# The last attention of four: PV with the probabilities as the stationary operand, and the division behind it

## The chip, the core and the metric

The kernel runs on one core of one Trainium2 chip. The metric is the device time of one launch in microseconds. Five engines work side by side: PE (TensorE), DVE (VectorE), ACT (ScalarE), POOL (GpSimd) and SP (SyncE, which issues the DMAs).

## The reference, cut to what matters

Four cross-attention layers run one after the other on `x` (8, 128, 256) and a context of the same shape. The change touches only the fourth, which has 16 heads of width 16, 128 queries and 128 keys for each of 8 sequences:

```python
x = layer_norm(hidden_states, ln1_w, ln1_b)
q = (x @ q_w + q_b).reshape(B, LQ, H, HD).transpose(0, 2, 1, 3)
k = (encoder_hidden_states @ k_w + k_b)...
v = (encoder_hidden_states @ v_w + v_b)...
scores = jnp.einsum('bhqd,bhkd->bhqk', q, k) * scale
scores = jnp.where(mask, scores, mask_value)
attn = jax.nn.softmax(scores, axis=-1)
out = jnp.einsum('bhqk,bhkd->bhqd', attn, v)
out = out.transpose(0, 2, 1, 3).reshape(B, LQ, D)
out = out @ cproj_w + cproj_b
hidden = out + residual
y = layer_norm(hidden, ln2_w, ln2_b)
y = jax.nn.gelu(y @ fc_w + fc_b, approximate=True)
return hidden + (y @ proj_w + proj_b)
```

Everything is in float32. Dense products are made from a rounded high part and a low part of each operand, three matmuls per product (`three`, L762 to L766).

## The kernel before, in words

Every engine has a program of its own and walks the same list of events; semaphores tie the engines together. The list of the fourth layer ("L3") is written by `att_order("L3")` (L171 to L248). Its unit u is one S event: four heads of one sequence. There are 32 units: 4 iterations (two sequences each) of 4 steps (four heads) of 2 units (the sequence). In the order of a unit u, for w = u - 5:

- S(u): PE makes the scores of four heads in one of two PSUM banks (L895 to L901), DVE takes the negated row maximum (L1609), ACT takes exp per head, with the row sum in its accumulator (L1270), DVE takes the reciprocal of the sums (L1560, for the unit before), and POOL multiplies the 128x512 probabilities by it (L1857).
- T(u - 3): PE transposes the four heads (L909), ACT (even) or DVE (odd) copies them to `probT` (L1281, L1622).
- PV(w): PE multiplies, four products of a stationary 128x32 slice of the values (`vt`, 16 columns of it filled) and 128 moving columns of `probT`, into the 32-row strips of an output bank (L932). The result is transposed already, channels in rows.
- OUT(it), right behind the last PV of an iteration: ACT copies the bank to the high part `uu[0]` (L1287), DVE writes the low part (L1625).
- WO(it), two units later (`WO_LATE`; directly in the next unit after the last iteration): PE makes the output projection in a general bank, DVE adds it to the residual `X` and takes the statistics of the next norm (L1631, L1481).
- For the next steps: "pq" and "pk" (stacked queries and keys, L851 to L861, copied by ACT L1252 and L1262 and DVE L1606, the other key rows by DMA L679), and for the next iteration "dk", "dq", "dv" in units 3, 5 and 9 of an iteration (dense projections; ACT L1246, DVE L1578, values DVE L1592).
- Then further events, written with `put` (L191 to L207): parts of the MLP weights ("w", ACT L1201, DVE L1471), the norm in front of the MLP ("nS", "nX", "nT"), and the first MLP groups: ("up", 0, 0) in unit 32, ("up", 0, 1) in unit 33, ("up", 0, 2) in unit 36. An "up" is 12 matmuls on PE, a gelu on ACT (L1365), and the high and low parts on DVE (L1713, L1714).

Dense products, stackings, projections and norm transposes ("general" users) share two PSUM banks in turn (`j_bank`, `j_take`). The waits for a bank to be freed sit in PE's program ahead of the user's first matmul. DVE walks the list through `late` (L260 to L275): up to the last S, the kinds named in `LATE["L3"]` are done behind the next S event; after the last S the list holds as written. `SEAM_COVER` fills PE with matmuls on the identity ahead of a norm's transposes; only `norm_step` calls `cover` (L786).

The MLP of the layer follows ("L3" of `mlp_order`, L366 to L375): ("up", 0, 3), ("up", 1, 0), the first "down" and the second half of the norm, which needs the WO of all iterations.

## Time and profile before

| | us |
|---|---|
| median of 3 runs | 1174.37 (1172.15 to 1174.82) |
| the profiled execution's own time | 1175.04 |
| its span in the trace | 1173.2 |
| PE busy | 1062.5 (91%) |
| DVE busy | 727.7 (62%) |
| ACT busy | 715.2 (61%) |
| POOL busy | 317.5 (27%) |

The span is what the trace covers; the execution's own time has 1.8 us around it. The shares are means over four layers with different limits, so a change in one layer is read from that layer's stretch. The fourth layer's first S runs near 1016 us, its last PV at 1119.5 us, and its MLP ends the program. In the views, a busy PE counts a matmul up to its modelled end, so matmuls that follow each other overlap in the records. In a timeline the columns are start, duration, engine, line, operation, output and input names, shape and count; a bracket gives the idle time before and what ended it.

### The profile page before, as it was taken

The page shows a single profiled execution, that of the slowest core. Times are in us where ns is not written, and L with a number is a line of the kernel's source. Part 1 is how long each engine was busy: PE and PEld are TensorE (multiplying, and loading weights), DVE is VectorE, ACT ScalarE, POOL GpSimd, SP SyncE. Part 2 cuts the span into 40 slices and gives each one's busy share as a digit, 9 for nine tenths or more (in the row PEclk, how much of TensorE's full clock was granted, in tenths as well). Part 3 has the DMA queues.
Part 4 walks back from the last instruction along what each step waited for, and adds up shares of the span by engine and source line. Part 5 has one row for each costly group of instructions (what it writes and reads, how often), then busy time and mean ns, then how long its engine had stood idle before and what let it go on. Part 6 is the DMA issues. An engine that isn't in the chain of part 4 may idle for free.

```text
span 1173.2 us, 24063 instructions
## 1 busy us (share of the span) xinstructions
PE 1062.5 (91%) x8248; PEld 936.7 (80%) x8248; DVE 727.7 (62%) x1747; ACT 715.2 (61%) x2080; POOL 317.5 (27%) x440
## 2 busy tenths in 40 slices
PE   7998897789978999999998989999999989778788
PEld 5776675677758979999998868999998979667588
DVE  7777574667886645555555645555555585667773
ACT  2776765677884456666655546666665452689852
POOL 5232543756540012211111103111112112143311
PEclk9999899899999999999999999999999999899899
DMA  5211011011101021111001101011111110100100
GB/s 171 66 46 41 22 43 33 15 23 27 45 20 53 19 90 46 46 46 46 19 29 68 46 1 57 35 46 46 46 46 37 37 54 1 48 18 19 48 10 28
DMA packets 29853, 48.09 MB, mean 41 GB/s; under 512 B 6627, under 2 KB 20389, under 8 KB 29734
## 3 DMA queue, kind: packets, MB, share of 16 engines
q1 hardware_dynamic: 29638, 46.49, 12.7%
q8 instruction: 68, 1.11, 0.4%
q14 instruction: 51, 0.42, 0.1%
q10 hardware_dynamic: 96, 0.07, 0.0%
HBM read 36.54 MB, written 1.05 MB: 32 GB/s over the span
## 4 chain that ended last, share of the span: by engine, by line
PE 66%; DVE 12%; ACT 10%; issue 7%; POOL 2%; SPq 1%; DMA 1%; ACTq 0%; DVEq 0%; POOLq 0%
PE ps L764 14%; PE ps L765 14%; PE ps L766 14%; PE ps L1008 4%; PE ps L984 4%; PE ps L1146 3%; ACT pt L1270 2%; PE ps L993 2%; PE ps L909 2%; DVE nm L1806 2%; PE ps L1133 1%; PE ps L1124 1%; PE ps L932 1%; DVE nmax L1609 1%; POOL pt L1857 1%
## 5 line engine op out<-in xcount | busy, mean ns | idle before, releaser
L1857 POOL TENSOR_TENSOR pt<-pt,prec 128x256 f32<-128x256 f32 (+1 forms) x224 | 180.8, 808 | 628.2 <-DVE prec L1678 500.4
L1325 ACT ACTIVATE pt<-ps,nmax 128x129 f32<-128x129 f32 x256 | 92.1, 366 | 101.0 <-DVE nmax L1670 100.2
L764 PE MATMUL ps<-rs 128*128 128x256 f32 x480 | 142.8, 298 | 4.1 <-DVE rs L1692 2.8
L1471 DVE TENSOR_TENSOR rs<-wraw,rs 128x256 fp32r<-128x256 f32 (+2 forms) x116 | 68.8, 595 | 124.5 <-ACT rs L1201 124.1
L765 PE MATMUL ps<-rs 128*128 128x256 f32 x480 | 135.9, 283 | 0.0
L766 PE MATMUL ps<-rs 128*128 128x256 f32 x480 | 135.8, 283 | 0.0
L1270 ACT ACTIVATE pt<-ps,nmax 128x256 f32<-128x256 f32 (+1 forms) x256 | 105.1, 423 | 42.6 <-DVE nmax L1609 42.3
L764 PE MATMUL ps<-ht,rs 128*128 128x256 f32 (+1 forms) x304 | 107.6, 354 | 9.0 <-DVE ht L1521 3.0
L766 PE MATMUL ps<-ht,rs 128*128 128x256 f32 (+1 forms) x304 | 101.4, 333 | 0.0
L765 PE MATMUL ps<-ht,rs 128*128 128x256 f32 (+1 forms) x304 | 101.3, 333 | 0.0
L764 PEld LDWEIGHTS ps<-rs 128*128 128x128 f32 x480 | 91.8, 191 | 7.9 <-DVE rs L1692 4.8
L1692 DVE SCALAR_TENSOR_TENSOR rs<-ps,col,rs 128x256 fp32r<-128x256 f32 x128 | 61.9, 484 | 53.1 <-ACT rs L1342 53.1
L765 PEld LDWEIGHTS ps<-rs 128*128 128x128 f32 x480 | 92.0, 192 | 0.0
L766 PEld LDWEIGHTS ps<-rs 128*128 128x128 f32 x480 | 91.9, 191 | 0.0
L764 PE MATMUL ps<-rs,ct 128*128 128x256 f32 x288 | 86.4, 300 | 3.4 <-ACT rs L1252 1.5
L1806 DVE TENSOR_REDUCE nm<-ps 128x2 f32<-128x512 f32 x128 | 82.1, 679 | 7.0 <-PE ps L1124 7.0
L1609 DVE TENSOR_REDUCE nmax<-ps 128x2 f32<-128x512 f32 (+1 forms) x96 | 65.6, 684 | 29.3 <-PE ps L899 21.9
L984 PEld LDWEIGHTS ps<-fs 128*128 128x128 f32 x512 | 75.7, 190 | 10.1
L1365 ACT ACTIVATE fs<-ps,col 128x256 f32<-128x256 f32 x96 | 40.2, 471 | 68.4 <-PE ps L766 67.3
L1413 ACT ACTIVATE pt<-ps 128x512 f32<-128x512 f32 x128 | 73.1, 599 | 14.2 <-PE ps L1133 12.2
L765 PE MATMUL ps<-rs,ct 128*128 128x256 f32 x288 | 80.9, 281 | 0.0
L766 PE MATMUL ps<-rs,ct 128*128 128x256 f32 x288 | 80.9, 281 | 0.0
(206 smaller groups left out, 2998.8 us busy)
## 6 DMA issues: line engine op xcount, KB each, us to landing
wraw<-in_packs SPq DMA_DIRECT2D x52, 512.0 KB, 3.8
rs<-rs SPq DMA_DIRECT2D x222, 32.0 KB, 1.9
bvr<-in_l2rows SPq DMA_DIRECT2D x16, 256.0 KB, 4.6
rs<-rs SPq DMA_DIRECT2D x96, 16.0 KB
row<-in_rows SPq DMA_DIRECT2D x2, 640.0 KB, 4.9
XH<-in_packs SPq DMA_DIRECT2D x2, 512.0 KB, 4.0
out<-X SPq DMA_DIRECT2D x4, 256.0 KB, 2.1
X<-in_x SPq DMA_DIRECT2D x3, 256.0 KB, 3.3
```

The source lines that it names most:

```text
L764: nc.tensor.matmul(dst, w[0], m[1], start=start, stop=False)
L765: nc.tensor.matmul(dst, w[1], m[0], start=False, stop=False)
L766: return nc.tensor.matmul(dst, w[0], m[0], start=False, stop=stop)
L984: last = nc.tensor.matmul(ps[:, S_BANK + g % 2, b * D:b * D + P + 1], qT[:, hh % 3, 2 * b2 + b, :], kT[:, hh % 3, 2 * b2 + b, :], start=Tr ...
L1270: last = nc.scalar.activation(prob[:, i % PROBS, h * keys:(h + 1) * keys], ps[:, SCORE_BANKS[ph][i % len(SCORE_BANKS[ph])], h * keys:(h + ...
L1325: last = nc.scalar.activation(prob[:, g % PROBS, k * D:k * D + P + 1], ps[:, S_BANK + g % 2, k * D:k * D + P + 1], ACT.Exp, bias=nmax[:, g ...
L1413: nc.scalar.activation(pt[:, i % L0_PTS, :], ps[:, L0_X[i % len(L0_X)], :], ACT.Exp, scale=Q0_SCALE).then_inc(Z["ex"], 1)
L1471: last = nc.vector.tensor_tensor(dst[1], src, f32(dst[0]), ALU.subtract)
L1609: nc.vector.tensor_reduce(nmax[:, i % 4, 0:nh], ps[:, SCORE_BANKS[ph][i % len(SCORE_BANKS[ph])], :].rearrange("p (h n) -> p h n", h=nh), A ...
L1692: nc.vector.scalar_tensor_tensor(cc[1][:, hd, two, :], ps[:, O_BANK + g % 2, 0:D].rearrange("p (b n) -> p b n", b=2), C(f"L2bv{p // PAIRS ...
L1806: nc.vector.tensor_reduce(nm[:, s % 3, im, 2 * p:2 * p + 2], ps[:, L0_S[i % len(L0_S)], :].rearrange("p (h n) -> p h n", h=2), AX.X, ALU.m ...
L1857: nc.gpsimd.tensor_tensor(pr, pr, prec[:, u % 4, 0:nh].unsqueeze(2).broadcast_to([P, nh, keys]), ALU.mult)\
```

## The change

The row sum is no longer taken by ACT and no longer divided out before the transposes. T waits for exp. The values get a column of ones behind their 16 columns. In PV `probT` of a head (128 keys x 128 queries) is the stationary operand and 17 columns of `vt` move; the result has queries in rows and holds the row sum as its 17th column. A new event NO, one unit behind every second PV, is done by DVE: a reciprocal of 8 sums per row and one multiplication of two sequences' four heads into `attn`. OUT becomes four transposes of `attn` on PE into a general bank, in front of ACT's copy and DVE's subtraction; it is two units later than before for the first three iterations and one unit later, behind the last NO, for the last. WO is two units later for the first three iterations, one unit for the last. POOL waits for exp ahead of its row additions. Two entries of `SEAM_COVER` go.

```diff
-SEAM_COVER = {("nT", "L2nm", 0): 5, ("nT", "L2nm", 2): 6, ("pq", "L3", 0): 6, ("S", "L3", 2): 9}
+SEAM_COVER = {("nT", "L2nm", 0): 5, ("nT", "L2nm", 2): 6}
...
             yield ("PV", w // U)
-            if w % per_it == per_it - 1:
+            if ph == "L1" and w % per_it == per_it - 1:
                 yield ("OUT", w // per_it)
+        if ph == "L3" and 2 <= w <= total and w % 2 == 0:
+            yield ("NO", w // 2 - 1)
+        for it in range(c["iters"] if ph == "L3" else 0):
+            if w == (it + 1) * per_it + (2 if it + 1 < c["iters"] else 0):
+                yield ("OUT", it)
...
-            if w == (it + 1) * per_it + ((WO_LATE if ph == "L3" else 1) if it + 1 < c["iters"] else 0):
+            if w == (it + 1) * per_it + (4 if ph == "L3" and it + 1 < c["iters"] else 1 if ph == "L3" or it + 1 < c["iters"] else 0):
                 yield ("WO", it)
...
+        def sums(s):
+            return ps[:, O_BANK + s % 2, 0:2 * P].rearrange("p (m q c) -> p m q c", m=2, q=4)
...
-                    pe.wait_ge(a["nm"], i + 1)
+                    pe.wait_ge(a["nm" if ph == "L1" else "ex"], i + 1)
...
+                elif e == "PV" and ph == "L3":
+                    it, r = divmod(i, 2 * STEPS)
+                    m, im = divmod(r, 2)
+                    copied(pe, ph, i)
+                    if r == 0:
+                        pe.wait_ge(a["vals"], it + 1)
+                    if i >= 4 and im == 0:
+                        pe.wait_ge(a["nm"], i // 2 - 1)
+                    for q in range(4):
+                        last = nc.tensor.matmul(sums(i // 2)[:, im, q, 0:HD + 1], probT[:, i % 3, q * P:(q + 1) * P],
+                                                vt[:, it % 2, im, 0, 4 * m + q, 0:HD + 1], start=True, stop=True)
+                    last.then_inc(a["pm"], 1)
+                elif e == "OUT" and ph == "L3":
+                    pe.wait_ge(a["nm"], STEPS * (i + 1))
+                    bank = j_bank()
+                    for im in range(2):
+                        for t in range(2):
+                            last = nc.tensor.transpose(bank[:, (2 * im + t) * P:(2 * im + t + 1) * P], attn[:, i % 2, im, t * P:(t + 1) * P],
+                                                       ident[:, :])
+                    j_full(last, (a["oeA"], i + 1), (a["oeD"], i + 1))
...
+                            last = nc.scalar.activation(p_h, s_h, ACT.Exp, bias=nmax[:, i % 4, h:h + 1])
...
+                        if ph == "L3":
+                            last = nc.vector.tensor_tensor(vt[:, i % 2, s, 0, :, 0:HD],
+                                                           bank[:, s * D:(s + 1) * D].rearrange("p (h d) -> p h d", d=HD),
+                                                           R("L3v").rearrange("p (h d) -> p h d", d=HD), ALU.add)
+                            continue
...
-                    if i >= 1:
+                    if ph == "L1" and i >= 1:
                         reciprocal(i - 1)
...
+                elif e == "NO":
+                    it, m = divmod(i, STEPS)
+                    dve.wait_ge(a["pm"], 2 * i + 2)
+                    if m == 0 and it >= 2:
+                        dve.wait_ge(a["oeA"], it - 1)
+                    rc = prec[:, 2 * (i % 2):2 * (i % 2) + 2, 0:4]
+                    link(nc.vector.reciprocal(rc, sums(i)[:, :, :, HD]))
+                    dst = attn[:, it % 2, :, m // 2 * P:(m // 2 + 1) * P].rearrange("p m (q e d) -> p e m q d", q=4, e=2)[:, m % 2, :, :, :]
+                    nc.vector.tensor_tensor(dst, sums(i)[:, :, :, 0:HD], rc.unsqueeze(3).broadcast_to([P, 2, 4, HD]),
+                                            ALU.mult).then_inc(a["nm"], 1)
...
                 if e == "S":
-                    normalise(a, i, 4 // U, keys, keys)
+                    if ph == "L1":
+                        normalise(a, i, 4 // U, keys, keys)
...
                     if ph == "L3" and 1 <= i <= B:
+                        pool.wait_ge(a["ex"], i)
                         add_row(X, "L3o", i - 1)
...
-                part = nc.gpsimd.memset(fs[:, 512 * b:512 * (b + 1)], 0.0)
-            part.then_inc(vzero, 1)
+                if b < 2:
+                    ones = nc.gpsimd.memset(vt[:, b, :, 0, :, HD], 1.0)
+                if b == 1:
+                    ones.then_inc(vzero, 1)
```

## Rows read from the trace of the kernel before

**Rows 1.** Busy time by window over the last attention and the start of its MLP.
```profile
core 0: us, PE busy (x) PEld busy (x) DVE busy (x) ACT busy (x) POOL busy (x), PEclk, DMA share, GB/s
1027.00:1098.30 71.30, 60.28 (x577) 48.58 (x575) 50.49 (x122) 62.31 (x255) 30.41 (x32) 1.00 0.12 27
1098.30:1102.60 4.30, 0.07 (x5) 0.07 (x1) 3.21 (x8) 4.29 (x16) 1.04 (x1) 0.74 0.02 5
1102.60:1119.50 16.90, 12.85 (x116) 10.38 (x116) 12.94 (x23) 12.02 (x38) 3.49 (x3) 0.86 0.09 32
```

**Rows 2.** Timeline of PE: a stall, and one unit without.
```profile
1059.97 0.74 PE L851 MATMUL ps<-rs,sel 128*128 128x256 f32 x4 [1.32 <-DVE rs L1578]
...
1061.15 0.60 PE L909 MATMUL ps<-ident,pt 128*128 128x128 f32 x4
1061.68 0.42 PE L932 MATMUL ps<-pt,fs 128*32 128x128 f32 x8
1062.04 0.38 PE L764 MATMUL ps<-rs 128*128 128x256 f32 x1
```

**Rows 3.** Groups by line and shape, 1027 to 1098.3: busy us, mean ns, idle before.
```profile
L1857 POOL TENSOR_TENSOR pt<-pt,prec 128x512 f32<-128x512 f32 x25 | 26.0, 1040 | 40.1 <-DVE prec L1560 40.1
L1270 ACT ACTIVATION_READ_ACCUMULATOR pt<-ps,nmax 128x1 f32 x97 | 20.0, 206 | 0.0
...
L932 PE MATMUL ps<-pt,fs 128*32 128x128 f32 x200 | 10.6, 285 | 0.0
...
L1560 DVE RECIPROCAL prec<-psums 128x4 f32<-128x4 f32 x25 | 4.2, 168 | 0.3 <-ACT pt L1270 0.3
...
L1592 DVE TENSOR_TENSOR fs<-ps,row 128x128 f32<-128x128 f32 x12 | 2.6, 275 | 0.0
```

**Rows 4.** Timeline of the weight loads, at 39.8 us and at 706.6 us.
```profile
39.81 0.30 PEld L1114 LDWEIGHTS ps<-rs 128*128 128x128 f32 x2 [0.66 <-issue]
...
706.59 0.53 PEld L1008 LDWEIGHTS ps<-pt,fs 128*128 128x128 f32 x4
```

**Rows 5.** Timeline of ACT: exp of two heads of one unit.
```profile
1062.07 0.37 ACT L1270 ACTIVATE pt<-ps,nmax 128x128 f32<-128x128 f32 x1
1062.34 0.19 ACT L1270 ACTIVATION_READ_ACCUMULATOR pt<-ps,nmax 128x1 f32 x1
1062.43 0.36 ACT L1270 ACTIVATE pt<-ps,nmax 128x128 f32<-128x128 f32 x1
```

**Rows 6.** Timeline of DVE and POOL: one form alone, and beside a division.
```profile
1051.29 0.41 DVE L1520 CAST ht<-XH 128x512 fp32r<-128x512 f32 x1
...
1108.96 1.41 POOL L1857 TENSOR_TENSOR pt<-pt,prec 128x512 f32<-128x512 f32 x1 [0.75 <-DVE prec L1560]
...
1109.39 1.26 DVE L1520 CAST ht<-XH 128x512 fp32r<-128x512 f32 x1
```

**Rows 7.** Timeline of ACT, DVE and PE around the stall at 1098.3.
```profile
1100.68 0.60 ACT L1287 CAST rs<-ps 128x512 fp32r<-128x512 f32 x1
...
1101.31 0.69 DVE L1625 TENSOR_TENSOR rs<-ps,rs 128x512 fp32r<-128x512 f32 x1 [0.30 <-ACT rs L1287]
...
1102.56 0.77 PE L899 MATMUL ps<-rs 128*128 128x256 f32 x2 [4.23 <-DVE rs L1606]
```

**Rows 8.** Timelines of PE, ACT and DVE from the last PV to the last WO.
```profile
1119.52 0.43 PE L932 MATMUL ps<-pt,fs 128*32 128x128 f32 x8 [2.31 <-DVE pt L1622]
1121.84 0.41 PE L764 MATMUL ps<-rs 128*128 128x256 f32 x1
...
1120.02 0.59 ACT L1287 CAST rs<-ps 128x512 fp32r<-128x512 f32 x1 [2.43 <-PE ps L932]
1122.08 0.84 ACT L1365 ACTIVATE fs<-ps,col 128x256 f32<-128x256 f32 x2 [1.48 <-PE ps L766]
...
1122.95 0.43 DVE L1713 CAST rs<-fs 128x512 fp32r<-128x512 f32 x1 [1.63 <-ACT fs L1365]
1123.41 1.11 DVE L1714 TENSOR_TENSOR rs<-fs,rs 128x512 fp32r<-128x512 f32 x1
```

More of the change, by code:

```diff
@@ L33 @@
 H = 16
+HD = D // H
 DK2 = 128
@@ L81 @@
 PROBS = 4
-WO_LATE = 5 - T_LAG
 TE_ACT = {"L1": 2, "L3": 2}
@@ L512, in build @@
         assert o2 <= o
+        attn, _ = carve(fs, o, [2, 2, D])
         ms, o = carve(fs, o, [2, B, D])
@@ L1269, in att @@
                     for h in range(nh):
-                        last = nc.scalar.activation(prob[:, i % PROBS, h * keys:(h + 1) * keys],
-                                                    ps[:, SCORE_BANKS[ph][i % len(SCORE_BANKS[ph])], h * keys:(h + 1) * keys], ACT.Exp,
-                                                    bias=nmax[:, i % 4, h:h + 1], accum_out=psums[:, i % 4, h:h + 1])
+                        p_h = prob[:, i % PROBS, h * keys:(h + 1) * keys]
+                        s_h = ps[:, SCORE_BANKS[ph][i % len(SCORE_BANKS[ph])], h * keys:(h + 1) * keys]
+                        if ph == "L1":
+                            last = nc.scalar.activation(p_h, s_h, ACT.Exp, bias=nmax[:, i % 4, h:h + 1], accum_out=psums[:, i % 4, h:h + 1])
+                        else:
+                            last = nc.scalar.activation(p_h, s_h, ACT.Exp, bias=nmax[:, i % 4, h:h + 1])
                     last.then_inc(a["ex"], 1)
@@ L1282, in att @@
                 elif e == "OUT":
-                    act.wait_ge(a["pm"], 2 * STEPS * (i + 1))
-                    bank = ps[:, OUT_BANKS[ph][i % len(OUT_BANKS[ph])], :]
+                    if ph == "L1":
+                        act.wait_ge(a["pm"], 2 * STEPS * (i + 1))
+                        bank = ps[:, OUT_BANKS[ph][i % len(OUT_BANKS[ph])], :]
+                    else:
+                        bank = j_take()
                     if i > 0:
@@ L1585, in att @@
                     for s in range(2):
-                        im, t = (k[0], s) if ph == "L1" else (s, 0)
+                        if ph == "L3":
[3 more added lines that the diff above has]
+                            continue
+                        im, t = k[0], s
                         src = bank[:, s * D:(s + 1) * D].rearrange("p (t e q d) -> p e t q d", t=2, e=2, q=4)
@@ L1610, in att @@
                                             AX.X, ALU.max, negate=True).then_inc(a["mx"], 1)
-                    if i >= 1:
+                    if ph == "L1" and i >= 1:
                         reciprocal(i - 1)
-                    if i == total - 1:
+                    if ph == "L1" and i == total - 1:
                         reciprocal(i)
+                elif e == "NO":
[8 more added lines that the diff above has]
+                                            ALU.mult).then_inc(a["nm"], 1)
                 elif e == "T":
@@ L1623, in att @@
                 elif e == "OUT":
+                    bank = ps[:, OUT_BANKS[ph][i % len(OUT_BANKS[ph])], :] if ph == "L1" else j_take()
                     dve.wait_ge(a["oeA"], i + 1)
-                    nc.vector.tensor_tensor(uu[1].rearrange("p m t n -> p (m t n)"), ps[:, OUT_BANKS[ph][i % len(OUT_BANKS[ph])], :],
+                    nc.vector.tensor_tensor(uu[1].rearrange("p m t n -> p (m t n)"), bank,
                                             f32(uu[0].rearrange("p m t n -> p (m t n)")), ALU.subtract).then_inc(a["oeD"], 1)
@@ L1871, in att @@
                 if e == "S":
-                    normalise(a, i, 4 // U, keys, keys)
+                    if ph == "L1":
+                        normalise(a, i, 4 // U, keys, keys)
                     if ph == "L1" and i in (4, 14):
```

## The prediction

> **What bounds the kernel now.** I looked first at the table of windows over the last attention [rows 1]. In its steady part (1027 to 1098.3 us) ACT is busy 62.3 of 71.3 us, PE 60.3, DVE 50.5, POOL 30.4, at the full TensorE clock (1.00): no engine is saturated, and ACT is nearest. PE has 71.3 - 60.3 = 11.0 us of idle there. The reader should see two near-bounds side by side: relief for ACT is worth something only as far as PE has room, and work added to PE is free only as far as it falls into those 11.0 us. The PE timeline shows how a unit runs: four transposes (L909), PV (L932), then dense or stacking matmuls, back to back until a bank is missing; the last row of the group is one such stall, 1.32 us for DVE's low part of the dense projection (L1578) [rows 2]. None of these stalls ends with POOL: POOL waits for the reciprocal, and T is issued three units behind S, so the division on POOL (1.04 us a unit [rows 3]) is hidden.
>
> **PE: PV with the probabilities stationary.** Both versions issue four products a unit, and the profile has two records for each (200 L932 records for 25 units [rows 3]). Before, eight records on 32-column tiles overlap: from the first transpose (1061.15) to the first matmul behind PV (1062.04) is 0.89 us, of which the four transposes, 0.60 us less one record of some 0.28 for three of them, are 0.43 to 0.44; so PV costs 0.45 [rows 2]. After, each record has a 128-column weight load and only 17 moving columns. No row has 17 columns. The nearest are 128 columns: a pair of weight loads of L1114 takes 0.30 us with 0.19 for one, so they follow each other at 0.11; four of L1008, the same operand type as here, follow at (0.53 - 0.19) / 3 = 0.113 [rows 4]. L1114 streams half the columns of its neighbours and gets no closer together, so I read this as the price of the load, not of the stream. I take 8 x 0.109 = 0.87 us, just under these: 0.42 more per unit. The bounds are 8 x 0.12 = 0.96 above, and the old 0.45 below (no dearer at all).
> The Trainium skill ("TensorE: Matmul & The Clock Gate", section Back-to-back issue gap) puts a matmul of 1 to 64 columns at some 25 ns; by that alone PV would take about 0.2 us and the change would relieve PE. The same page's section LDWEIGHTS prices a load by its columns, 128 / 1.2 = 107 ns, which is what the rows of weight loads show; these govern here.
> The new OUT step is four transposes, 0.44 us, in each of four iterations, and it takes a general bank.
>
> **ACT.** Exp of one head starts at 1062.07, its accumulator read at 1062.34, the next head's exp at 1062.43: the read takes a slot of 0.09 us [rows 5], which goes with it. Per unit that is 4 x 0.09 = 0.35 us less. Bounds: 0 and 0.8 (the whole 0.206 of the accumulator rows, four times [rows 3]).
>
> **DVE and POOL.** Removed: 32 reciprocals of 0.17 us, two per step. Added per step: a reciprocal (0.17), a linked wait (some 0.1), a 128x128 multiplication from PSUM (0.28, as L1592) [rows 3]. So DVE gains about 0.2 us a step of work and loses its waits for exp; the values' bias goes from four instructions to two. I cost all this at nothing in the steady part, covered by PE; if DVE were the bound it would be 16 x 0.2 = 3.2. The queue position is what matters at the end, below. POOL's 1.04 us divisions go: DVE's L1520 takes 0.41 us alone and 1.26 where a division lies beside it [rows 6], so each such meeting gives back up to 0.85.
> The Trainium skill ("SBUF — State Buffer", section SBUF: two separate sides) says that GpSimd and such VectorE instructions exclude each other on a shared pair of ports for a whole instruction; the trace agrees (1.26 against 0.41). It speaks for the change, and only where DVE holds the path.
> The later T wait (exp in place of the division), POOL's added wait for exp before its row additions (nothing urgent queues behind it), the two small memsets instead of eight (POOL was idle there), and the two deleted cover entries, whose events never call that function, cost 0.
>
> **The sum,** against the profiled execution of 1175.04 us:
> - Steady part: 25 PV x 0.42 + 2 OUT x 0.44 = +11.4 us of PE work. What falls into the 11.0 us of idle is free. Most stalls are a wait for ACT or DVE with a PV between cause and effect, so each absorbs 0.42, plus 0.35 where an exp stands ahead of the copy that frees the bank. I take 9.0 absorbed, net +2.4 (bounds: half absorbed, +5.9; all, +0.4).
> - WO of an iteration now falls in the same unit as the next dv, two dense groups on two banks: +0.3 (0 to 1.8, a stall of 0.9 twice).
> - The stall at 1098.3: its chain on ACT loses one exp saving (0.35) and the OUT copy (0.60), on DVE the OUT subtraction [rows 7]: -1.2 (0 to -2.2, if PE then keeps its clock, 0.74 in this stretch and 0.86 in the next [rows 1]).
> - 1102.6 to 1119.5: five or six dearer PVs and an OUT against its idle of 4 us (16.9 - 12.85 [rows 1]) and one meeting with POOL less (-0.85): +0.8 (-1.5 to +3).
> - The end. The last PV is issued in unit 36, followed by the third MLP group ("up", 0, 2), whose conversion on DVE waits for its gelu. Before, OUT of the last iteration stood ahead of that: ACT's copy (1120.02) and DVE's subtraction were done while PE ran the MLP group, and WO started at once (1121.84) [rows 8]. After, the division ("NO", 15) and OUT are listed in unit 37. DVE is in order, so the division waits behind L1713 and L1714, which wait for the gelu: from the end of the MLP group, gelu ready 1.1 us on, conversions to 1124.52, 2.7 us on [rows 8]; then division 0.6, PE transposes with their latency 0.7, ACT copy 0.6, subtraction 0.7. WO starts 5.3 us behind the group instead of 0. All of the later MLP stands behind WO on PE, so it all moves. Plus 0.4 for the PV, less 0.7 for a weight conversion that now fits into the wait: +5.0 (+3 to +7, as PE may restart at half clock).
> Total 2.4 + 0.3 - 1.2 + 0.8 + 5.0 = +7.3: 1182.3. The median before is 0.67 below the profiled execution, so I forecast **1181.7 us**.
>
> **Rivals.**
> (A) *ACT is the bound, and the end is covered.* For it: ACT has the highest share [rows 1]. Then PE's stalls shrink further. PE's own work limits it: the 60.3 us hold at each stall a matmul's tail of some 0.17 us (a record of 0.28 less a spacing of 0.11); with some 19 stalls that is 3.2, so 57.1 + 11.4 = 68.5 is the least for the steady part, -2.8. With -2.2 at the stall, -1.5 after it and only +3.0 at the end, -3.5: 1170.9. It decides if the stalls vanish altogether; against it stand the waits for DVE, which gets no relief. 0.10.
> (B) *The short matmuls are cheap* (the issue rule above): PV at about 8 x 0.06 = 0.48, PE gains nothing and loses nothing. Then the steady part gains about half of ACT's 25 x 0.35 = 8.8, -4.4; with -1.2, -0.8 and +4.6 the sum is -1.8: 1172.6. Against it: the weight loads [rows 4]. 0.08.
> (C) *The gain and the loss cancel,* end +3, the rest 0 to -3: 1174 to 1177. 0.09.
> (D) *The clock.* With PV's streaming shortened and a 4 us hole at the end, PE falls to 1.2 GHz in part of the attention; each 5 us of PE work at that level costs 5 more. The clock held 1.00 through the steady part with 11 us idle, and fell only around the 4.3 us hole [rows 1]. +15 or more: above 1189. 0.05.
> (E) The forecast, slower by work on PE and by the late division: 0.68.
>
> **Numbers.** About 0.2% (2.3 us) is what a measurement of this kernel can tell from no change. Faster takes most of (A) and (B) and some of (C): 0.15; same 0.10; slower 0.75. The range leaves out (D) and the far side of (A): 1172.5 to 1189.5. Its lower part is B's and C's, its upper part the bounds of the steady part and the end.
>
> **What would show it.** PE's PV group at 0.85 to 0.95 us a unit (right) or near 0.45 (B); no accumulator reads in the last attention, ACT's exp at 0.26 a head; the PE idle of the steady part down from 11 to 2 to 4 us and its length up by 2 to 3; the stall near 1098 a microsecond shorter; and, clearest, a hole on PE of four to five microseconds in front of the last WO, ended by the OUT copy and subtraction, with DVE's multiplication started only after the third gelu's conversion. If that hole is missing, or PV stays at 0.45, the prediction is wrong.

## The result, and the profile after

| | before | after |
|---|---|---|
| median, us | 1173.26 (4 runs) | 1190.16 (4 runs, 1188.77 to 1196.17) |
| ratio to before | | 1.0156 [1.0115, 1.0198] |
| the profiled execution's own time | 1175.04 | 1191.27 |
| its span | 1173.2 | 1189.5 |
| mean granted TensorE clock | 0.978 | 0.967 |

The changed kernel is 16.9 us slower; 8.4 were forecast against this median, and the upper end of the range (1189.5) is missed by 0.7. The work around the change is the same, but some line numbers move: L764 to L766 of before are L773 to L775, L851 is L860, L858 is L867, L899 (S) is L908, L909 (T) is L918, L1287 is L1322, L1365 (gelu) is L1400, L1578 is L1613, L1592 is L1622, L1625 is L1675, L1713 and L1714 are L1763 and L1764. PV is L930, NO's reciprocal and multiplication L1660 and L1662, OUT's transposes L938.

The first view to read is the table of windows of the changed kernel, cut where the clock changes. Its columns are those of [rows 1].

```profile
core 0: us, PE busy (x) PEld busy (x) DVE busy (x) ACT busy (x) POOL busy (x), PEclk, DMA share, GB/s
1023.50:1033.00 9.50, 7.73 (x63) 7.25 (x63) 5.44 (x10) 7.42 (x21) 2.21 (x3) 0.99 0.07 14
1033.00:1046.30 13.30, 13.30 (x65) 13.30 (x64) 5.74 (x12) 6.39 (x18) 0.98 (x1) 0.50 0.08 16
1046.30:1105.20 58.90, 54.89 (x459) 53.23 (x458) 41.30 (x94) 42.78 (x118) 0.00 (x0) 1.00 0.11 26
1105.20:1107.20 2.00, 0.11 (x2) 0.01 (x1) 1.85 (x5) 2.00 (x7) 0.00 (x0) 1.00 0.00 0
1107.20:1121.50 14.30, 14.29 (x71) 14.29 (x72) 7.35 (x14) 10.12 (x25) 0.00 (x0) 0.53 0.11 38
1121.50:1128.50 7.00, 5.84 (x50) 5.75 (x50) 5.69 (x13) 2.07 (x5) 0.00 (x0) 0.99 0.00 0
1128.50:1142.10 13.60, 9.14 (x40) 8.45 (x41) 4.02 (x9) 2.46 (x5) 2.03 (x2) 0.50 0.01 1
```

Two things are new against [rows 1]. PE is busy 54.89 of 58.9 us in the longest piece (93%, before 85%), while ACT's share falls from 87% to 73% and POOL has nothing to do: PE alone bounds the kernel now. And PE runs at 0.50 (1.2 GHz) in three stretches of 13.3, 14.3 and 13.6 us. Before, the only dips in the stage lay in its start, behind the stall of 4.2 us and near the last WO. The first new one is the strangest line of the table: PE is busy for the whole 13.30 us and still gets 1.2 GHz. Before, PE came out of its stall of 4.23 us at half clock too, but had the full clock back after 4.64 us of work (1102.56 to 1107.20).

The PE timeline shows a unit at either clock, the slow one first. The first two lines are what PE did just before the clock fell: two short waits, 0.44 and 0.48 us.

```profile
1030.98 0.74 PE L860 MATMUL ps<-rs,sel 128*128 128x256 f32 x4 [0.44 <-DVE rs L1613]
...
1032.56 0.86 PE L807 MATMUL ps<-ident,XH 128*128 128x128 f32 x4 [0.48 <-ACT rs L1281]
...
1033.65 1.05 PE L918 MATMUL ps<-ident,pt 128*128 128x128 f32 x4
1034.50 1.73 PE L930 MATMUL ps<-fs,pt 128*128 128x17 f32 x8
1036.07 0.77 PE L908 MATMUL ps<-rs 128*128 128x256 f32 x2
...
1058.97 0.60 PE L918 MATMUL ps<-ident,pt 128*128 128x128 f32 x4
1059.41 0.96 PE L930 MATMUL ps<-fs,pt 128*128 128x17 f32 x8
...
1062.42 0.96 PE L930 MATMUL ps<-fs,pt 128*128 128x17 f32 x8
1063.23 0.63 PE L938 MATMUL ps<-ident,fs 128*128 128x128 f32 x4
1063.62 0.36 PE L908 MATMUL ps<-rs 128*128 128x256 f32 x1
```

PV's eight records last from 1062.42 to 1063.23, 0.81 us (0.87 forecast, 0.45 before), or 0.101 for each. The 0.45 of before was worked out differently: there the transposes (L909) and PV together take 0.89 us from start to start, and here 0.44 (1058.97 to 1059.41) and 0.81, 1.25 in all. So a unit's pair costs 0.36 more at the full clock, where 0.42 was forecast. At half clock the same eight last from 1034.50 to 1036.07, 1.57 us. OUT's four transposes cost 0.39 (0.44 forecast). So each PV that falls into a slow stretch costs 0.76 more, beside everything else there.

ACT's timeline has the exponentials of four heads in one row without accumulator reads, 1.14 us in all (0.257 from head to head; the forecast was 0.26):

```profile
1059.90 1.14 ACT L1304 ACTIVATE pt<-ps,nmax 128x128 f32<-128x128 f32 x4
```

The last view is the tail, from the last PV to the last WO, on PE, ACT and DVE. It answers to [rows 8].

```profile
1128.53 1.89 PE L930 MATMUL ps<-fs,pt 128*128 128x17 f32 x8 [1.19 <-DVE pt L1671]
...
1133.21 0.84 ACT L1400 ACTIVATE fs<-ps,col 128x256 f32<-128x256 f32 x2 [6.61 <-PE ps L775]
1134.08 0.43 DVE L1763 CAST rs<-fs 128x512 fp32r<-128x512 f32 x1 [5.16 <-ACT fs L1400]
...
1134.54 1.09 DVE L1764 TENSOR_TENSOR rs<-fs,rs 128x512 fp32r<-128x512 f32 x1
1135.55 0.20 DVE L1660 RECIPROCAL prec<-ps 128x8 f32<-128x8 f32 x1
1135.78 0.29 DVE L1662 TENSOR_TENSOR fs<-ps,prec 128x128 f32<-128x128 f32 x1
...
1136.13 1.12 PE L938 MATMUL ps<-ident,fs 128*128 128x128 f32 x4 [2.96 <-DVE fs L1662]
1137.28 0.58 ACT L1322 CAST rs<-ps 128x512 fp32r<-128x512 f32 x1 [3.24 <-PE ps L938]
1137.97 0.69 DVE L1675 TENSOR_TENSOR rs<-ps,rs 128x512 fp32r<-128x512 f32 x1 [1.90 <-ACT rs L1322]
...
1138.72 0.58 PE L773 MATMUL ps<-rs 128*128 128x256 f32 x1 [1.47 <-DVE rs L1675]
```

This is the late division as forecast: DVE idles 5.16 us for the third gelu, though the last PV has ended at 1130.42, converts the gelu (1134.08 to 1135.55), and only then divides. PE has holes of 2.96 and 1.47 us, and WO starts 5.5 us behind the end of the MLP group (1136.13 - 2.96 = 1133.17 to 1138.72; 5.3 forecast). The group before it and the WO behind it run at 1.2 GHz.

A difference that is not in the sum: the fourth layer starts earlier, its first stacking matmul at 1010.63 instead of 1013.75. That is not the change's doing as far as the runs can tell: in the other traces this matmul starts at 1008.8 to 1011.3 us where the fourth layer is the old one, and at 1008.1 to 1012.2 where it is the new one. POOL's eight memsets of 128x512 in the third layer's MLP have become two small ones; what that is worth doesn't stand out from this spread. To keep chance out, the stages are compared from that matmul on.

### The profile page after: what moved, and what is told of

The parts are those of the page before. It is cut to its first block, busy times and chain, and to the rows that moved or that the text cites. A ratio compares the mean times of both kernels' runs of the same rounds, so it can differ in the third digit from the quotient of the medians.

```text
span 1189.5 us, 23913 instructions
## 1 busy us (share of the span) xinstructions
PE 1087.4 (91%) x8264; PEld 975.2 (82%) x8264; DVE 727.6 (61%) x1739; ACT 706.7 (59%) x1952; POOL 282.5 (24%) x402
## 4 chain that ended last, share of the span: by engine, by line
PE 69%; DVE 13%; ACT 8%; issue 6%; POOL 2%; DMA 1%; SPq 1%; ACTq 0%; DVEq 0%; POOLq 0%
PE ps L773 14%; PE ps L775 14%; PE ps L774 14%; PE ps L1037 4%; PE ps L1013 4%; PE ps L1175 3%; PE ps L918 2%; PE ps L1022 2%; PE ps L930 2%; DVE nm L1856 2%; PE ps L1162 1%; PE ps L1153 1%; DVE nmax L1648 1%; PE ps L807 1%; POOL pt L1907 1%
## 5 line engine op out<-in xcount | busy, mean ns | idle before, releaser
L1907 POOL TENSOR_TENSOR pt<-pt,prec 128x256 f32<-128x256 f32 (+1 forms) x192 | 147.2, 767 | 563.3 <-DVE prec L1728 500.4
L773 PE MATMUL ps<-rs 128*128 128x256 f32 x480 | 142.8, 298 | 5.0 <-DVE rs L1742 2.8
L775 PE MATMUL ps<-rs 128*128 128x256 f32 x480 | 135.9, 283 | 0.0
L773 PE MATMUL ps<-ht,rs 128*128 128x256 f32 (+1 forms) x304 | 107.8, 355 | 7.1 <-DVE ht L1556 2.9
L775 PE MATMUL ps<-ht,rs 128*128 128x256 f32 (+1 forms) x304 | 101.3, 333 | 0.0
L773 PEld LDWEIGHTS ps<-rs 128*128 128x128 f32 x480 | 91.8, 191 | 8.4 <-DVE rs L1742 4.8
L775 PEld LDWEIGHTS ps<-rs 128*128 128x128 f32 x480 | 91.9, 191 | 0.0
L773 PE MATMUL ps<-rs,ct 128*128 128x256 f32 x288 | 86.8, 302 | 1.8 <-ACT fs L1343 1.4
L1400 ACT ACTIVATE fs<-ps,col 128x256 f32<-128x256 f32 x96 | 40.2, 471 | 78.9 <-PE ps L775 78.6
L1937 POOL TENSOR_TENSOR X<-X,row 128x256 f32<-128x256 f32 x48 | 40.1, 842 | 191.1 <-ACT fs L1400 167.0
L775 PE MATMUL ps<-rs,ct 128*128 128x256 f32 x288 | 81.5, 283 | 0.0
```

Of the source, the lines that this page charges most:

```text
L773: nc.tensor.matmul(dst, w[0], m[1], start=start, stop=False)
L775: return nc.tensor.matmul(dst, w[0], m[0], start=False, stop=stop)
L1907: nc.gpsimd.tensor_tensor(pr, pr, prec[:, u % 4, 0:nh].unsqueeze(2).broadcast_to([P, nh, keys]), ALU.mult)\
```

## The experiments

Fourteen kernels ran, each beside runs of the kernel before on the same chip (their medians were 1172.2 to 1172.5 us). All differences below are against those.

| kernel | median, us | ratio to before [95%] |
|---|---|---|
| e0_after: the changed kernel again | 1186.58 | 1.0120 [1.010, 1.014] |
| e1_cols64: PV moves 64 columns | 1179.34 | 1.0061 [1.0037, 1.0085] |
| e2_end: third MLP group behind the division | 1183.42 | 1.0088 [1.0069, 1.0107] |
| e4_both: e1 and e2 | 1174.50 | 1.0019 [1.0006, 1.0032] |
| e6_order: e4, more of the MLP later | 1175.00 | 1.0019 [1.0008, 1.0031] |
| e10_dv: e4, values' projection a step earlier | 1171.63 | 1.0003 [0.9985, 1.0020] |
| e8_fill: e10 and PE kept at work in the tail | 1170.33 | 0.9983 [0.9971, 0.9996] |
| e15_fill_s: e8 and the same ahead of an S | 1173.62 | 1.0006 [0.9988, 1.0023] |
| e3_before_noacc: before, no row sums on ACT | 1166.97 | 0.9946 [0.9926, 0.9966] |
| e5_before_17: before, PV moves 17 columns | 1170.72 | 0.9988 [0.9977, 0.9999] |
| e7_before_fill: before, 10.6 us of PE work added | 1175.90 | 1.0030 [1.0017, 1.0042] |
| e9_before_17x4: e5, each PV product four times | 1176.71 | 1.0037 [1.0025, 1.0049] |
| e13_before_loads: e5, full weight loads added | 1185.64 | 1.0127 [1.0104, 1.0149] |
| e12_fill_t: the changed kernel, dense matmuls added | 1186.58 | 1.0125 [1.0105, 1.0146] |

### The clock: the same kernel, and 64 columns instead of 17

> The changed kernel as it is, beside the three variants. Its trace has PE at 1.2 GHz in three stretches of the last layer (13.3 us inside the attention, 14.3 behind the stall of the square roots, 13.6 at the end). If these come from the new PV (clock theory), they are there again, some 35 us or more at the lower level in all, and the ratio to the kernel before is 1.012 to 1.020. If they were chance, this run has fewer of them and a ratio near 1.006, the +7.3 us of the forecast.

The changed kernel again took 1186.58 us, 3.6 less than in the first measurement. In its trace the slow stretch of the attention lies elsewhere: 1025 to 1090 is at 1.00, then comes this, in the PE timeline:

```profile
1089.99 0.96 PE L930 MATMUL ps<-fs,pt 128*128 128x17 f32 x8
1091.19 0.71 PE L860 MATMUL ps<-rs,sel 128*128 128x256 f32 x4 [0.24 <-DVE X L1681]
1092.76 0.47 PE L867 MATMUL ps<-rs,sel 128*128 128x256 f32 x2 [0.87 <-DVE fs L1622]
...
1093.19 0.59 PE L908 MATMUL ps<-rs 128*128 128x256 f32 x2
1093.58 1.06 PE L918 MATMUL ps<-ident,pt 128*128 128x128 f32 x4
1094.43 1.73 PE L930 MATMUL ps<-fs,pt 128*128 128x17 f32 x8
```

A PV, two short waits of 0.24 and 0.87 us, and from the S at 1093.19 on everything is slower: the transposes grow from 0.60 to 1.06, PV from 0.96 to 1.73. PE then works without a gap at 0.51 until 1114, 20.8 us. The low level adds up to some 31 us behind 1025 (an estimate from the granted clock of the windows), not quite the 35 expected, and the ratio is at the low edge of its band. The profiled execution of the first measurement met the same two waits at 1097.5 and kept its clock. Where it falls differs from one execution to the next; that it falls somewhere in the attention is common to both traces, and to e2_end's below. All five falls in these three attentions begin right behind waits of PE of 0.24 to 1.90 us, and the low level then lasts 10 to 21 us although PE has no gap in it.

```diff
-return ps[:, O_BANK + s % 2, 0:2 * P].rearrange("p (m q c) -> p m q c", m=2, q=4)
+return ps[:, O_BANK + s % 2, :].rearrange("p (m q c) -> p m q c", m=2, q=4)
...
-last = nc.tensor.matmul(sums(i // 2)[:, im, q, 0:HD + 1], probT[...],
-                        vt[:, it % 2, im, 0, 4 * m + q, 0:HD + 1], start=True, stop=True)
+nhd = 2 if 4 * m + q < H - 1 else 1
+last = nc.tensor.matmul(sums(i // 2)[:, im, q, 0:32 * nhd], probT[...],
+                        vt[:, it % 2, im, 0, 4 * m + q:4 * m + q + nhd, :]..., start=True, stop=True)
```

> PV moves 64 columns a product in place of 17 (32 for the last head); the further columns are never read. The weight loads stay. Clock theory (PE falls to 1.2 GHz because 17 columns leave the array nearly idle while weights load): the PV group stays at 0.81 us at full clock, the half-clock stretch inside the attention goes or shrinks, and the kernel is 4 to 12 us faster than the changed one. Rival (the clock falls for other reasons, such as the holes around it): same half-clock stretches, time within 2 us of the changed kernel. Rival (the moving columns are paid): PV at 0.9 us or more, 3 us slower.

It moves the next head's values too, which nobody reads. Measured: 1179.34 us, 7.2 less than e0_after, for nearly four times the moving columns. The windows:

```profile
1025.00:1090.00 65.00, 61.28 (x508) 59.14 (x509) 43.02 (x91) 47.84 (x139) 3.19 (x4) 1.00 0.11 26
1090.00:1120.00 30.00, 24.67 (x207) 23.62 (x205) 22.92 (x54) 20.42 (x49) 0.00 (x0) 1.00 0.08 23
1120.00:1131.00 11.00, 6.57 (x32) 6.23 (x32) 5.36 (x10) 2.74 (x6) 2.03 (x2) 0.69 0.01 1
```

and in its PE timeline the S behind the stall, the last PV and the last WO:

```profile
1101.03 0.51 PE L908 MATMUL ps<-rs 128*128 128x256 f32 x2 [1.86 <-ACT rs L1292]
...
1117.52 1.08 PE L931 MATMUL ps<-fs,pt 128*128 128x64 f32 x8 [1.18 <-DVE pt L1672]
...
1125.19 0.58 PE L773 MATMUL ps<-rs 128*128 128x256 f32 x1 [1.47 <-DVE rs L1676]
```

The attention now runs at 1.00 to its last PV, through the same waits as e0_after: 0.20 and 0.87 us at 1091.32 and 1092.89, where e0_after had 0.24 and 0.87 and lost its clock. So the waits alone don't lower it. It isn't the chance of one trace either: the mean granted clock of the four executions is 0.968 to 0.974 for e0_after and 0.977 to 0.981 here. A PV row is 1.00 us where it was 0.96, and at the full clock the next row starts 0.81 us behind it where it waits for nothing, as with 17 columns: the columns are free, the weight load sets the pace. This isolates the cost of the clock. Of the 7.2 us against e0_after, 5.8 have arisen by the last PV (112.9 us from the stage's start against 107.1) and 1.4 in the tail; in the first measurement it is 10.8 and 2.5 up to the last WO.

It also gives the forecast's own sum something to be compared with. Offsets are from the stage's first stacking matmul (1013.75, 1010.63, 1010.39):

| us from the stage's start | before | after | e1_cols64 |
|---|---|---|---|
| S behind the stall | 88.8 | 96.6 | 90.6 |
| last PV | 105.8 | 117.9 | 107.1 |
| last WO | 108.1 | 128.1 | 114.8 |
| end | 159.5 | 178.9 | 166.4 |

With the clock held in the attention, the stage is 7.0 us longer than before (166.41 against 159.45), against a forecast of 7.3; the changed kernel's own is 19.4.

### The end: the third MLP group moved behind the division

```diff
-    put(total + 4, "up", 0, 2)
+    put(total + (5 if ph == "L3" else 4), "up", 0, 2)
```

> Only the order of the end: the third MLP group moves from unit 36 to unit 37, behind the last division and OUT. Late-division theory: the hole of 3.4 + 2.3 us on PE in front of the last WO shrinks to one of about 1.5 in front of OUT; WO starts 4 to 5 us earlier, and with less time at 1.2 GHz behind it the kernel is 4 to 8 us faster than the changed one. Rival (the gelu and its conversions, now later, are the next thing waited for): the hole only moves, under 2 us gained.

> 64 moving columns and the order of the end together. If both theories hold and are independent, 8 to 18 us faster than the changed kernel: a ratio to the kernel before of 1.000 to 1.008. If only the end's order matters: 1.008 to 1.012. If the stretches at the end are the same ones that the columns cure, the sum is less than the two parts.

e2_end took 1183.42 us, 3.2 less than e0_after and so less than the 4 to 8 expected (6.7 against the first measurement); e4_both 1174.50, 4.8 less than e1_cols64. The tail of e2_end on DVE and PE:

```profile
1127.15 1.30 PE L930 MATMUL ps<-fs,pt 128*128 128x17 f32 x8 [1.19 <-DVE pt L1671]
...
1128.49 0.21 DVE L1660 RECIPROCAL prec<-ps 128x8 f32<-128x8 f32 x1 [0.96 <-PE ps L930]
1128.74 0.29 DVE L1662 TENSOR_TENSOR fs<-ps,prec 128x128 f32<-128x128 f32 x1
1129.08 1.11 PE L938 MATMUL ps<-ident,fs 128*128 128x128 f32 x4 [0.63 <-DVE fs L1662]
```

The division follows its PV by 1.3 us (before this edit 7.0: 1128.53 to 1135.55), and PE's waits of 2.96 and 1.47 become one of 0.63. That shows the queue position on DVE as the cause, and prices it: 4.8 us where the clock is held in the attention. e2_end still has 0.61 and 0.51 in two stretches of the attention (1030 to 1043 and 1097 to 1118), so the two causes are separate.

> The run with 64 columns and the late MLP group, and one thing more at the end: the second MLP group two list positions later (unit 34, behind the last T) and the first part of a weight conversion three units later, so that the copy of the last transposes no longer stands behind a gelu on DVE. Theory (the 1.2 us hole in front of the last PV is that queue): the hole goes, 1 to 3 us faster than e4, at or below the kernel before (0.998 to 1.001). Rival (the gelu groups are on the path and only swap with the hole): within 1 us of e4.

e6_order moves the second MLP group one unit further back as well, and part of a weight conversion three units. It took 1175.00: no gain over e4_both (1174.50), as its rival had it. The 1.18 us wait ahead of the last PV is gone, but PE's wait for the division behind it grows from 0.63 to 2.50.

### What the relief of ACT and the work on PE are worth, on the kernel before

```diff
+acc = {"accum_out": psums[:, i % 4, h:h + 1]} if ph == "L1" else {}
-bias=nmax[:, i % 4, h:h + 1], accum_out=psums[:, i % 4, h:h + 1])
+bias=nmax[:, i % 4, h:h + 1], **acc)
...
+nc.vector.memset(psums[:, :, :], 1.0)
```

> The kernel before, with the accumulator read of the last attention's exp left out (the row sums are then a constant 1, so the probabilities are not divided by their sums; the division itself still runs). ACT loses 0.35 us a unit, nothing else changes. PE-and-waits theory (ACT's relief is worth what the stalls behind exp give back): 2 to 5 us faster than before. Rival A of the prediction (ACT is the bound): 7 to 10 us faster. If ACT's relief were worthless: within 1 us.

The row sums are left out: the probabilities are multiplied by one. One of its four executions, the profiled one, took 2985 us, so its trace is not read; the other three took 1163.72, 1166.94 and 1167.01. Their median is 5.4 us less than before and the ratio makes it 6.3 (4.0 to 8.7), from 32 x 0.35 = 11.2 us less on ACT. So about half of the relief would reach the end, if PE were left as it was. That is just above the 2 to 5 expected and below the 7 to 10 of an ACT-bound kernel.

```diff
+if ph == "L3" and m >= 1:
+    if it >= 1:
+        pe.wait_ge(a["oeD"], it)
+    fill(ps[:, OUT_BANKS[ph][(it + 1) % 2], :], 2)
```

> The kernel before with two 128-column float32 matmuls on the identity behind 24 of the 32 PVs of the last attention, 0.44 us each time, 10.6 us of PE work in all, and nothing else. It tests the absorption that the prediction assumed (9.0 of 11.4 us). If PE's idle absorbs it as assumed: 1 to 4 us slower than before, at full clock. If PE is the bound: 8 to 11 us slower. If the stalls absorb everything: within 1 us.

`fill` multiplies the identity by itself; here it adds 0.44 us behind 24 of the 32 PVs, 10.6 us in all, and the clock stayed at 1.00 in the steady part. It took 1175.90, 3.6 more than before. PE's idle took in 7.0 us of 10.6, two thirds, where my sum let 9.0 of 11.4 vanish, four fifths. The interval of the ratio (2.0 to 4.9 us more) reaches from about a half to four fifths, so this run alone doesn't refute that share.

### What lowers the clock

```diff
-bank[32 * q:32 * q + 32, (m // 2) * P:(m // 2 + 1) * P], vt[...], probT[:, slot, c0:c0 + P]
+pc = P if ph == "L1" else HD + 1
+bank[32 * q:32 * q + 32, (m // 2) * P:(m // 2) * P + pc], vt[...], probT[:, slot, c0:c0 + pc]
```

> The kernel before, with PV of the last attention moving only 17 of its 128 columns (the other 111 queries of a head are left out). The 32-column weight loads stay. Clock theory (few streamed columns per time bring the granted clock down, not the form of the weights): the steady part shows stretches at 0.5, and in spite of less work the kernel is not faster, 0 to 8 us slower. Rival (only the long weight loads of the new form bring it down): clock 1.00 as before, PV at 0.2 to 0.3 us, 1 to 5 us faster.

In e5_before_17 the order of the kernel before stays, and PV computes only 17 of the 128 queries. It took 1170.72 us, 1.6 less than before, and its steady part stayed at the full clock:

```profile
1025.00:1090.00 65.00, 51.87 (x533) 45.03 (x532) 46.71 (x113) 56.76 (x238) 27.59 (x29) 1.00 0.12 27
```

17 columns alone don't lower the clock, not even with PE idle 13 of 65 us. e9_before_17x4 issues each of these products four times:

```diff
+for _ in range(0 if ph == "L1" else 3):
+    nc.tensor.matmul(bank[..., (m // 2) * P:(m // 2) * P + pc], vt[...], probT[:, slot, c0:c0 + pc],
+                     start=begin and t == 0, stop=False, skip_group_check=True)
```

> The kernel before with PV at 17 moving columns, 111 of 128 queries left out, and each such product issued four times, so that short matmuls fill PE for some 0.75 us a unit as in the changed kernel, still with 32-column weight loads. e5_before_17 (once each) took 1170.7 us and held 1.00. Theory 1 (what lowers the clock is PE's time spent on short matmuls, whatever their weights): granted clock 0.5 for some 15 to 25 us of 1027 to 1119 us, time 1183 to 1190 us. Theory 2 (it takes the full 128-column weight loads, or the full occupation of PE, which the dead time of the old order does not give): 1.00 through the steady part, time 1174 to 1178 us (25 x 0.55 us of work more, about two thirds of it absorbed).

```profile
1027.00:1099.00 72.00, 68.50 (x1165) 62.73 (x1164) 49.17 (x120) 61.49 (x245) 29.25 (x30) 1.00 0.12 27
```

1176.71 us and 1.00 throughout, at 95% PE busy: theory 2. Then the full weight load: e13_before_loads puts four products of the identity with 17 moving columns ahead of each unit's transposes.

```diff
+if ph == "L3":
+    for _ in range(4):
+        nc.tensor.matmul(ps[:, T_BANK + i % 2, 0:HD + 1], ident[:, :], ident[:, 0:HD + 1], start=True, stop=True)
```

> The kernel before with PV at 17 moving columns (111 of 128 queries left out, e5_before_17: 1170.7 us, 1.00 through the attention), and ahead of each unit's transposes four products of the identity as a full 128-column weight load with 17 moving columns, so 0.85 us a unit of the same loads as in the changed kernel's PV. Theory 1 (full weight loads with few columns behind each are what lowers the clock): granted clock 0.5 somewhere between 1027 and 1119 us for 10 us or more, and a time of 1185 us or more. Theory 2 (this pattern alone doesn't; it takes the changed kernel's order of work as well): 1.00 through that stretch and 1176 to 1182 us (27 us of PE work more than e5_before_17, of which some 18 fall into idle).

Its windows:

```profile
1027.00:1104.00 77.00, 75.28 (x774) 69.60 (x772) 51.40 (x125) 63.99 (x254) 30.30 (x31) 1.00 0.11 24
1104.00:1108.00 4.00, 1.17 (x17) 0.97 (x16) 2.43 (x6) 4.00 (x19) 1.04 (x1) 1.00 0.01 2
1108.00:1118.00 10.00, 10.00 (x62) 9.26 (x62) 6.52 (x13) 6.28 (x25) 3.49 (x3) 0.51 0.17 54
```

and the added loads in a unit of its PE timeline, with the transposes behind them:

```profile
1041.55 0.96 PE L911 MATMUL ps<-ident 128*128 128x17 f32 x8
1042.36 0.64 PE L913 MATMUL ps<-ident,pt 128*128 128x128 f32 x4
```

The added loads take 0.81 us a unit, exactly PV's price in the changed kernel. The clock criterion came out half and half: 1.00 for all of 1027 to 1104, as theory 2 has it, but behind the stall PE then works at 0.51 for ten microseconds without a gap, which is theory 1's 10 us or more at half clock; the kernel before had its clock back after 4.64 us of work behind the stall at this place. The time, 1185.64, lies above theory 2's band and in theory 1's; most of it is the 27 us of added work on a PE that has no idle left (75.28 of 77 us). The run doesn't decide between the two.

Last, the changed kernel with its 17 columns and two matmuls on the identity (0.44 us, 14 us in all) ahead of each unit's transposes:

```diff
+if ph == "L3":
+    fill(ps[:, T_BANK + i % 2, :], 2)
```

> The changed kernel, 17 columns as it is, with two 128-column matmuls on the identity (0.44 us) ahead of each unit's four transposes: 14 us of PE work more. Theory 1 (the clock falls because the share of time in which columns stream is too small): the attention runs at 1.00 from 1025 to its last PV; the stage grows by up to 14 us of work and wins back some 10 us of half clock, 1186 to 1191 us. Theory 2 (the 17-column form itself lowers the clock): half clock for as long as in the changed kernel or longer, 1197 us or more. Theory 3 (PE fully occupied is what lowers it): still longer at half clock, 1200 us or more.

```profile
1024.00:1106.00 82.00, 79.17 (x683) 77.91 (x681) 53.24 (x118) 57.23 (x162) 3.19 (x4) 1.00 0.10 23
1106.00:1124.00 18.00, 16.36 (x142) 16.14 (x142) 13.91 (x30) 12.59 (x31) 0.00 (x0) 1.00 0.09 30
1124.00:1137.00 13.00, 8.57 (x38) 7.88 (x39) 3.46 (x8) 2.46 (x5) 2.03 (x2) 0.50 0.00 1
```

1186.58 us, to the hundredth the median of e0_after, with 14 us of useless work more. The attention is at 1.00 to 1124; only the stretch with the tail's holes is left at 0.50. Theories 2 and 3, by which the 17-column form or a full PE by itself lowers the clock, would have had it at half clock for longer; they fall. One thing weakens the run: the added matmuls also shorten PE's waits (the 1.90 us ahead of the S behind the stall becomes 0.78), and the falls begin behind such waits. e1_cols64 has no such flaw, since its waits are e0_after's. Taken together, the slow stretches of the attention begin behind a short wait and last while PV moves 17 columns behind full weight loads; more columns in it keep the clock, and so does dense work beside it, if not by way of the shorter waits. That the share of time in which columns stream is what counts fits all of this, but no run measures it.

### A version that wins the loss back

```diff
-"L3": [(1 * 2 + 1, "dk", 0), (2 * 2 + 1, "dq", 0), (4 * 2 + 1, "dv", 0)]}[ph]
+"L3": [(1 * 2 + 1, "dk", 0), (2 * 2 + 1, "dq", 0), (3 * 2 + 1, "dv", 0)]}[ph]
```

> The version e4_both (1174.5 us) with the dense projection of the values moved one step earlier (to unit 7 of an iteration, before in 9), so that it no longer shares a unit with WO. Theory of the prediction (two dense groups on two banks in one unit stall PE, 0 to 1.8 us in all): the stalls of some 1.5 us on the stacking matmuls near 1073 and 1097.5 us go, and the time falls by 1 to 2 us, to 1172.5 to 1173.5. Rival (PE has no room, the wait is only moved to another bank user): 1174 to 1175.

The changed kernel's stall for WO and "dv" in one unit is the pair of waits shown above for e0_after (0.24 and 0.87, behind PV); in e10_dv those stacking matmuls follow PV without a wait. It took 1171.63 us, 2.9 less than e4_both by the medians, more than the 1 to 2 expected, though the intervals of the two ratios overlap. The forecast gave this stall 0.3 (bound 1.8).

```diff
+if i == 8 * c["iters"] - 1:
+    fill(ps[:, S_BANK, :], 5)
...
+if i + 1 == c["iters"]:
+    fill(ps[:, S_BANK, :], 3)
```

> The version with 64-column PV and the third MLP group moved back (e4_both, 1174.5 us), with five matmuls on the identity ahead of the last PV and three ahead of the last OUT's transposes, where PE waits. Theory (PE's clock falls behind a stretch with holes in the tail and costs what it runs slowly): the stretch behind 1115 us stays at 1.00 where e4_both has half clock for some 7 us, so 3 us off, 1171 to 1172. Rival (the level is not set by these waits, the fills only stand in the queue ahead of work that becomes ready): 1174.5 to 1176.5 and the same half clock.

The kernel that ran holds e10_dv's edit too, which its expectation doesn't mention; so it is to be compared with e10_dv. It took 1170.33 us, 1.3 less, with overlapping intervals again, and its ratio to before, 0.9983 [0.9971, 0.9996], is the only one of the repaired versions below one. Windows:

```profile
1098.00:1105.00 7.00, 6.41 (x43) 6.41 (x44) 5.20 (x11) 7.00 (x22) 0.00 (x0) 0.76 0.07 14
1105.00:1130.00 25.00, 24.47 (x203) 23.68 (x201) 17.80 (x40) 12.42 (x23) 4.11 (x4) 1.00 0.05 19
```

The tail is at 1.00, where e10_dv had 0.79 for 8 us. There is a slow piece at 1098 instead, behind PE's wait for ACT ahead of the next to last S (e10_dv has the same wait, 1.87 us, and kept its clock there). e15_fill_s fills that wait too:

```diff
+if ph == "L3" and i == 30:
+    pe.wait_ge(a["ex"], i - 1)
+    fill(ps[:, SCORE_BANKS[ph][i % 2], :], 7)
```

> The version of e8_fill (64-column PV, third MLP group behind the division, the values' projection a step earlier, eight matmuls on the identity in the tail; 1170.3 us) with seven more ahead of the next to last S, where PE waits 1.9 us for ACT and the clock then falls to 0.69 for 5 us. Theory (the fall follows that hole and costs PE time): 1.00 there and 1 to 1.5 us off, 1169 to 1169.5. Rival: the fall is not caused by that hole, or the fills delay the S: 1170.3 to 1171.5.

```profile
1097.96 1.83 PE L783 MATMUL ps<-ident 128*128 128x128 f32 x14 [1.05 <-ACT pt L1312]
1099.54 0.49 PE L911 MATMUL ps<-rs 128*128 128x256 f32 x2
```

The clock is 1.00 there, but the added matmuls could start only at 1097.96, and the S behind them starts at 1099.54, where e8_fill's started at 1098.59. The profiled executions are equal (spans 1169.0 and 1168.7), the median is 1173.62, above the bands of theory and rival alike: no gain. Since this kernel is nearly e8_fill and its interval reaches from 0.9988 to 1.0023, the best version's lead over the kernel before, 2 us by its median, is not safe.

## Why the prediction was wrong, point by point

The direction was right; the size was not: 16.9 us slower where 8.4 were forecast, and 14.4 in the second measurement, whose 1186.58 us would have lain inside the range. So the narrow miss of the range is partly a matter of which executions were drawn; that the slowdown was 1.7 to 2 times the forecast is not. The step that failed is the treatment of rival (D): "The clock held 1.00 through the steady part with 11 us idle, and fell only around the 4.3 us hole", hence a chance of 0.05 and nothing in the sum. It inferred from idle time that PE was far from losing its clock. But the PE of before filled its busy time with products of 128 and 256 columns; the change replaced the eight records of PV in each unit by 17-column ones behind full weight loads, and took the idle away at the same time. In the runs, half clock costs the changed kernel 12.5 us of its stage (178.9 against 166.4 with 64 columns), and 7.2 us in e0_after. What the sum missed is not that the clock falls behind a stall, which before showed, but that it falls behind waits of 0.24 to 1.90 us and does not come back for 10 to 21 us of gapless work. The mechanism and its price of "+15 or more" for (D) were near; the chance was not.

The Trainium skill ("TensorE: Matmul & The Clock Gate", Part 1 on the clock gate) says that the gate follows how busy the engine has been recently, and its section "Loop structure matters more than you think" wants the matmuls back to back. The trace agrees for the stretches behind holes in the tail and for where the falls of the attention begin, but not for how long they last: 13.30 of 13.30 us busy at 0.50. Someone who reads "busy" as the profile's busy share would have called this kernel safe.

That the sum of the other terms, +7.3, comes so near the 7.0 measured is partly luck, since errors inside it cancel. The terms, with e1_cols64 as the measure that leaves the attention's clock out:

- **PV at 0.87 us**: 0.81, and 0.36 more for transposes and PV together instead of 0.42. The weight load sets the pace, for 17 and for 64 columns alike. Rival (B) is out. The short issue gap of the Trainium skill ("TensorE: Matmul & The Clock Gate", Back-to-back issue gap) is not seen where each product brings its own full load: 0.101 us.
- **ACT's 0.35 us a unit**: right, 0.257 from head to head. Worth 5.4 to 6.3 us on the order of before (e3_before_noacc).
- **Steady part, WO beside "dv", and the stall**: +2.4, +0.3 and -1.2, together +1.5 at the S behind the stall; measured +1.8 (90.6 against 88.8). Inside it two errors cancel. The stall shrank from 4.23 to 1.86 us, -2.4, just beyond the far bound; so what lies ahead of it grew by 4.2, not 2.7. Over the same offsets PE's busy time rose from 60.3 to 70.0 us and its idle fell from 11.0 to 5.5: idle took in 5.5 us of 9.7, little more than half, where the sum had 9.0 of 11.4. WO beside "dv" has its part in this: the two pairs of waits make 2.0 us (0.20, 0.73, 0.20 and 0.87).
- **1102.6 to 1119.5**: +0.8; measured 1.3 - 1.8 = -0.5, inside the bounds. But before ran this piece at 0.86 and e1_cols64 at 1.00, which alone is worth up to 0.14 x 16.9 = 2.4 us (an estimate); work and waits grew.
- **The end**: +5.0; from the last PV to the last WO 7.7 us in e1_cols64 against 2.3 before, +5.4. The mechanism is as told, shown by e2_end and e4_both. In the changed kernel the same piece takes 10.2 us, since it runs at half clock.
- **Rival (A)**, ACT as the bound, fell: ACT waits 15.3 us for the row maximum between 1023.5 and 1105.2, and PE is nearly full.

Of the signs I had named, the clearest came out as written: a hole of 2.96 + 1.47 = 4.4 us in front of the last WO, with the multiplication behind the third gelu's conversion; so did exp at 0.26 a head. The others were right in direction and off in size: PV 0.81 (0.85 to 0.95), idle 5.5 us (2 to 4), steady part 4.2 longer (2 to 3), the stall 2.4 shorter (1). None of them asked for the granted clock in the steady part after.

**Open**: what exactly in the changed order keeps the clock low. Short products behind 32-column loads don't do it (e5 and e9 hold), dense work beside the new PV or the shorter waits that come with it cure it (e12), and e13 shows a long fall only behind a stall. Two executions of the changed kernel fall at different places and pass through the same waits elsewhere at 1.00, so it seems to sit at an edge. No run separates the later T wait or POOL's added wait from the rest.

## What to carry to other kernels

When a change turns the operands of a matmul round so that a full weight load serves few moving columns, add up not only its time but what the rest of the unit still gives PE to do; then look at the granted clock of the stage after, window by window, before looking for a stall. If the clock has fallen in a stretch in which PE is busy throughout, look at the waits just before it, and try moving more columns per load: they may be free. And a new step that is done by an in-order engine belongs ahead of whatever waits for a long chain on the same engine: one place later in the list cost 4.8 us here.

## What was not expected of the hardware

- PE without any idle at 1.2 GHz for 13.3 us, and 14.3 us more later, in one attention. The same order of work at 64 columns instead of 17 held 2.4 GHz.
- 17 and 64 moving columns cost the same 0.81 us per eight records behind 128-column float32 weight loads; the same 17 columns behind 32-column loads take 0.19 us for eight (e5_before_17).
- 14 us of useless dense matmuls in the attention cost the changed kernel nothing (1186.58 us with and without them): the attention then ran at 1.00 throughout.
- Behind a stall of 4.23 us the kernel before worked 4.64 us at half clock; the changed one, behind waits of 0.24 to 1.90 us, 10 to 21 us.
